# Tile shapes on TensorE in a two-block attention and convolution kernel: half-array score products, wide products as pairs of 64-column tiles

## The reference, cut to what matters

```python
# block 1, per image
xn  = layer_norm_over_channels(x_attn)            # first 48 of 192 channels
q, k, v = split(bn(w_qkv @ xn), (16, 16, 48))
attn = softmax(q.T @ k * 16**-0.5, axis=-1)       # 1024 x 1024
out  = v @ attn.T
y    = bn(w_proj @ relu(concat(out, x_skip)))
# block 2, per image
q, k, v = split(qkv_w @ x)                        # 8 heads of 24 channels
at   = softmax(l2norm(q) @ l2norm(k).T) @ v       # channel attention, 24 x 24 per head
conv = depthwise3x3(dw1 @ v)                      # conv1, conv2
t    = cp_in @ at                                 # 32 channels
cmap = cp_out @ (t * ci1(mean(t)) * ci2(t))       # 3x3, dilated 7x7, 1x1
smap = sp_out @ gelu_gate(depthwise3x3(sp_in @ conv))
y    = proj @ ((at + cmap) * sigmoid(smap) + conv * sigmoid(mean(cmap)))
```

## Time and profile before

| | |
|---|---|
| three timed runs | 395.29, 395.75, 396.08 us, median 395.75 |
| span of the profiled execution, first to last instruction | 393.8 us |
| what lies around the span, by the median | 1.95 us |
| PE busy, instructions | 353.9 us (90%), 2098 |
| DVE busy, instructions | 269.3 us (68%), 490 |
| ACT busy, instructions | 168.3 us (43%), 283 |
| POOL busy | 24.1 us |
| DMA | 12.37 MB, mean 31 GB/s |

### The profile page before, as it was taken

The page is one execution under the profiler, slowest core; times in us unless marked ns, Lnnn a source line. Parts: engine busy times, 40 slices in busy tenths (PEclk is TensorE's granted clock), DMA queues, the critical chain, the costliest instruction groups (busy, mean ns, idle before and its releaser), DMA issues.

```text
span 393.8 us, 5228 instructions
## 1 busy us (share of the span) xinstructions
PE 353.9 (90%) x2098; PEld 180.1 (46%) x2098; DVE 269.3 (68%) x490; ACT 168.3 (43%) x283; POOL 24.1 (6%) x29
## 2 busy tenths in 40 slices
PE   2978989999987998899999989998999889797995
PEld 1736644433465454544445465443244365352431
DVE  5757667551597647796878577889357889748553
ACT  2233054656503248346520775235522574625410
POOL 2030100000003200000000020000100001000000
PEclk9977689999997599999899999997999899969999
DMA  8450000000000001200002102000002111013005
GB/s 254 140 147 2 0 0 2 0 1 2 0 1 2 0 2 28 62 2 2 0 2 75 28 9 52 12 2 0 0 2 80 29 33 33 0 29 64 2 0 160
DMA packets 6069, 12.37 MB, mean 31 GB/s; under 512 B 2078, under 2 KB 2718, under 8 KB 5918
## 3 DMA queue, kind: packets, MB, share of 16 engines
q1 hardware_dynamic: 5532, 11.97, 11.2%
q10 hardware_dynamic: 514, 0.08, 0.1%
HBM read 5.32 MB, written 3.15 MB: 22 GB/s over the span
## 4 chain that ended last, share of the span: by engine, by line
PE 75%; ACT 7%; DVE 6%; SPq 4%; DMA 4%; POOL 2%; issue 1%; ACTq 0%
PE psO L616 5%; PE psR L791 5%; PE psA L606 4%; PE psA L587 3%; DVE nm L1374 2%; ACT pT L1980 2%; PE psB L659 2%; DMA x<-x_dram 2%; PE psB L680 2%; PE psS L616 2%; SPq L391 2%; DMA up<-up 2%; PE psA L564 2%; PE psA L791 2%; PE psO L544 2%
## 5 line engine op out<-in xcount | busy, mean ns | idle before, releaser
L1510 DVE SCALAR_TENSOR_TENSOR cx<-cpA,dw2w,cx 128x1024 f32<-128x1024 f32 x32 | 40.9, 1278 | 2.4 <-ACT cx L2012 2.4
L1521 DVE SCALAR_TENSOR_TENSOR dd<-spp,wt,dd 112x1024 f32<-112x1024 f32 x32 | 41.0, 1282 | 1.0 <-ACT dd L2093 0.3
L1980 ACT ACTIVATE pT<-psA 128x1024 f32<-128x1024 f32 x24 | 24.6, 1023 | 26.2 <-PE psA L606 26.0
L1374 DVE TENSOR_REDUCE nm<-psA 128x1 f32<-128x1024 f32 x20 | 24.5, 1223 | 12.2 <-PE psA L587 11.9
L616 PE MATMUL psO<-pT,vt 128*64 128x512 f32 x96 | 28.7, 678 | 0.1
L1510 DVE SCALAR_TENSOR_TENSOR cx<-cpB,dw2w,cx 128x512 f32<-128x512 f32 x32 | 23.8, 743 | 0.5 <-ACT cx L2012 0.5
L791 PE MATMUL psR<-up,wb 128*32 128x256 f32 (+1 forms) x336 | 20.9, 383 | 1.4 <-DMA up<-up 1.3
L606 PE MATMUL psA<-qs,ks 98*128 98x512 f32 x48 | 19.4, 488 | 2.1 <-ACT pT L1980 1.4
L587 PE MATMUL psA<-ks,qs 96*128 96x512 f32 x40 | 15.0, 456 | 3.2 <-DVE nm L1374 1.9
L606 PEld LDWEIGHTS psA<-qs,ks 98*128 98x128 f32 x48 | 8.1, 209 | 19.8 <-ACT pT L1980 16.2
L1310 DVE BATCH_NORM_STATS2 st<-x 128x6 f32<-128x512 f32 x24 | 15.7, 684 | 1.8 <-DMA x<-x_dram 1.6
(11 more groups left out here) (423 smaller groups left out, 735.9 us busy)
## 6 DMA issues: line engine op xcount, KB each, us to landing
up<-up SPq DMA_DIRECT2D x12, 200.0 KB, 3.1
x<-x_dram SPq DMA_DIRECT2D x4, 512.0 KB, 6.5
out_dram<-x SPq DMA_DIRECT2D x8, 256.0 KB, 2.1
wt<-params_dram SPq DMA_DIRECT2D x1, 1151.5 KB, 8.5
tp<-tp SPq DMA_DIRECT2D x8, 136.0 KB, 2.4
x<-x_dram SPq DMA_DIRECT2D x8, 128.0 KB, 5.0
out_dram<-x SPq DMA_DIRECT2D x8, 128.0 KB, 2.4
wt<-params_dram SPq DMA_DIRECT2D x1, 213.5 KB, 2.6
```

The costliest lines, as they stand in the source:

```text
L1374: v.tensor_reduce(s.nm[:, t:t + 1], score_ps[b][t % 2][:], AX_X, ALU.max, negate=True).then_inc(nm_s.of(b), 1)
L1510: v.scalar_tensor_tensor(acc, img, dw2w[:, blk, tap:tap + 1], acc, ALU.mult, ALU.add).then_inc(cv_s.of(c), 1)
L1521: v.scalar_tensor_tensor(acc, t.spp[:, dy:dy + HH, dx:dx + WW], par("w_spdw")[:, tap:tap + 1], acc, ALU.mult, ALU.add).then_inc(dv_s.of(c), 1)
L1980: a(s.pT[t % 2][:], s.scoreT_ps[:], ACT.Exp).then_inc(ex_s.of(b), 1)
```

## The change

Three things are done.

SP's order changes in one place: the stores of images 0 and 1 go behind `shift_u(1)` and `shift_t(2)`.

First, q and k are laid on 50 rows of each half of the array (rows 0 to 49 and 64 to 113): 2 rows for the maximum and 3 x 16 for high, low and high parts. q's half g holds the queries of pixels g x 512 and up, 512 columns; k stands in full in both halves. The two products of a `scores_t` step then lie in different array halves and write different banks. `score_rows` of images 2 and 3 does the same; of images 0 and 1 both products of a step use one half, and the next step the other. High and low parts are made on all rows at once by marks (`marks`, `mkb`) instead of on row slices. `row_max` of images 2 and 3 takes two partial maxima, and `split_max` joins them.

Second, `columns` issues each product with 128 (or 112) stationary columns as two products with 64.

Third, the 64-row parts of the projections become steps of their own (`_b`), as do the folded channels (`_last`), and all orders are listed anew.

```diff
+            def columns(o, w, x, start=True, stop=True):
+
+                half = o.shape[0] // 2
+                for j in range(2):
+                    p = slice(j * half, (j + 1) * half) if o.shape[0] == P else slice(j * SP2, min((j + 1) * SP2, o.shape[0]))
+                    last = mm(o[p], w[:, p], x, start=start, stop=stop, skip_group_check=True)
+                return last
...
+        def packed(g):
+            return slice(g * SP2, g * SP2 + 2 + 3 * QK)
...
-            t.qs = sb(f"qs_{i}", [P, N], F32R, on=on)
+            t.qs = sb(f"qs_{i}", [P, HB], F32R, on=on)
...
+            def q_product(b):
...
                 for n in range(2):
                     p = slice(n * SP2, n * SP2 + PD)
-                    last = mm(ps[0:CH, n * HB:(n + 1) * HB], w[p, :], s.xn[p, :], start=True, stop=True)
+                    last = mm(q_ps[b][rows(n), :], qw[p, rows(n)], s.xn[p, :], start=True, stop=True)
...
-            def score_rows(b, t):
...
-                for n in range(2):
-                    last = mm(ps[:, n * HB:(n + 1) * HB], s.qs[0:CH, t * P:(t + 1) * P],
-                              s.ks[0:CH, n * HB:(n + 1) * HB], start=True, stop=True)
+            def score_rows(b, j):
...
+                o = slice((j // 2) * P, (j // 2 + 1) * P)
+                if b < 2:
+                    p = packed(j % 2)
+                    for n in range(2):
+                        last = mm(score_ps[b][j % 2][:, n * HB:(n + 1) * HB], s.qs[p, o], s.ks[p, n * HB:(n + 1) * HB],
+                                  start=True, stop=True)
+                else:
+                    for g in range(2):
+                        p = packed(g)
+                        last = mm(psA[:, g * HB:(g + 1) * HB], s.qs[p, o], s.ks[p, (j % 2) * HB:(j % 2 + 1) * HB],
+                                  start=True, stop=True)
...
             def scores_t(b, t):
...
-                for n in range(2):
-                    last = mm(ps[:, n * HB:(n + 1) * HB], s.ks[0:CH + 2, t * P:(t + 1) * P],
-                              s.qs[0:CH + 2, n * HB:(n + 1) * HB], start=True, stop=True)
+                for g in range(2):
+                    p = packed(g)
+                    last = mm(ps[:, g * HB:(g + 1) * HB], s.ks[p, t * P:(t + 1) * P], s.qs[p, :], start=True, stop=True)
...
                 for v in range(2):
-                    mm(o[:, v, :, 0:4], gav[:, 0, v, :], s.mv[:, :, 0:4], start=True, stop=True)
-                    last = mm(o[:, v, :, 4:6], gav[:, 1, v, :], s.mv[:, :, 4:6], start=True, stop=True)
+                    columns(o[:, v, :, 0:4], gav[:, 0, v, :], s.mv[:, :, 0:4])
+                    last = columns(o[:, v, :, 4:6], gav[:, 1, v, :], s.mv[:, :, 4:6])
...
             def k_low(b):
...
-                v.scalar_tensor_tensor(s.ks[64:96, :], k_ps[64:96, :], bqk[64:96, 1:2], s.ks[64:96, :].bitcast(F32),
+                v.scalar_tensor_tensor(s.ks[:], k_ps[:], bkq[:, 0:1], s.ks[:].bitcast(F32),
...
             def max_copy(b):
...
-                a(s.qs[CH:CH + 2, :], s.max_ps[0:2, :], ACT.Copy).then_inc(qm_s.of(b), 1)
+                for g in range(2):
+                    a(s.qs[g * SP2:g * SP2 + 2, :], s.max_ps[0:2, g * HB:(g + 1) * HB], ACT.Copy).then_inc(qm_s.of(b), 1)
```

The orders, the few places that the prediction speaks of:

```diff
 # ACT
+            setup_ln()
             load_small()
-            setup_ln()
-            zero_front(0)
-            zero_back(0, 0)
...
 # DVE
+            setup_slot1()
             setup_zeros()
...
+            setup2_a()
+            group_stats(0, 0)
...
-            channel_stats(0, 2, 0)
             layer_norm(0)
...
             row_max(0, 4)
+            channel_stats(0, 2, 0)
+            row_max(0, 5)
```

More of the change, by code:

```diff
@@ L481, in setup_bias @@
                 pe.wait_ge(*gmm[0](0, 1))
[L482 to L483 removed]
+                for k, w in enumerate((kw, qw)):
+                    last = mm(psS[:, 500 + k:501 + k], w[:], par("pick_one"), start=True, stop=True)
                 last.then_inc(s_pe, 1)
@@ L535, in pixel_var @@
                 for t in range(4):
-                    last = mm(s.row_ps[:, 2 * t:2 * t + 2], s.sq[:, t * P:(t + 1) * P], par("mean_rows"),
-                              start=True, stop=True)
+                    last = columns(s.row_ps[:, 2 * t:2 * t + 2], s.sq[:, t * P:(t + 1) * P], par("mean_rows"))
                 last.then_inc(var_s.of(b), 1)
@@ L658, in conv1_a, with conv1_b, conv1_last @@
                 for n in range(2):
-                    mm(front.F[n], wc1[:, 0:P], pair[c % 2].X[:, n, :], start=True, stop=False)
+                    columns(front.F[n], wc1[:, 0:P], pair[c % 2].X[:, n, :], stop=False)
+            def conv1_b(c):
                 for n in range(2):
-                    last = mm(front.F[n], wc1B[rows(n), 0:P], pair[c % 2].X[rows(n), 2, :], start=False, stop=True)
+                    last = mm(front.F[n], wc1B[rows(n), 0:P], pair[c % 2].X[rows(n), 2, :], start=False, stop=True,
+                              skip_group_check=True)
                 last.then_inc(c1_s.of(c), 1)
-            def conv1_b(c):
+            def conv1_last(c):
                 pe.wait_ge(*ce_s(c, 1))
@@ L679, in gram_x @@
                 for k in range(NKT):
-                    last = mm(front.F[0][:, 0:C], front.xT[:, k, 0:P], front.xT[:, k, :], start=(k == 0), stop=(k == NKT - 1))
+                    last = columns(front.F[0][:, 0:C], front.xT[:, k, 0:P], front.xT[:, k, :], k == 0, k == NKT - 1)
                 last.then_inc(gp_s.of(c), 1)
@@ L689, in gram_w @@
                 for k in range(2):
-                    last = mm(front.F[0][:, 0:2 * C], front.gram[:, k, 0:P], wq[:, k, :], start=(k == 0), stop=(k == 1))
+                    last = columns(front.F[0][:, 0:2 * C], front.gram[:, k, 0:P], wq[:, k, :], k == 0, k == 1)
                 last.then_inc(tup_s.of(c), 1)
@@ L714, in k_norm_rows @@
                 for h in range(2):
-                    last = mm(front.F[1][0:CH, h * CH:(h + 1) * CH], ones[0:CH, :], front.dk[:, h, :], start=True, stop=True)
+                    for j in range(2):
+                        last = mm(front.F[1][rows(j), h * CH:(h + 1) * CH], ones[0:CH, 0:SP2], front.dk[:, h, :],
+                                  start=True, stop=True)
                 last.then_inc(kr_s.of(c), 1)
@@ L837, in attended_a, with attended_b @@
                 for n in range(2):
-                    mm(t.R[TAIL[n]], pair[c % 2].wmt[:, 0:P], pair[c % 2].X[:, n, :], start=True, stop=False, skip_group_check=True)
+                    columns(t.R[TAIL[n]], pair[c % 2].wmt[:, 0:P], pair[c % 2].X[:, n, :], stop=False)
+            def attended_b(c):
+                t = back[SLOT2[c]]
+                pe.wait_ge(*pr_s(c, 1))
                 for odd in range(2):
@@ L865, in proj2_a, with proj2_last @@
                 for n in range(2):
-                    mm(t.R[TAIL[n]], wph[:, 0:P], t.uu[:, n, :], start=True, stop=False)
-                for n in range(2):
-                    last = mm(t.R[TAIL[n]], wphB[rows(n), 0:P], t.uu[rows(n), 2, :], start=False, stop=True)
-                last.then_inc(op_s.of(c), 1)
+                    columns(t.R[TAIL[n]], wph[:, 0:P], t.uu[:, n, :], stop=False)
             def proj2_b(c):
                 t = back[SLOT2[c]]
+                for n in range(2):
+                    last = mm(t.R[TAIL[n]], wphB[rows(n), 0:P], t.uu[rows(n), 2, :], start=False, stop=True, skip_group_check=True)
+                last.then_inc(op_s.of(c), 1)
+            def proj2_last(c):
+                t = back[SLOT2[c]]
+                pe.wait_ge(*zz_s(c, 3))
+                pe.wait_ge(*ae_s(c, 3))
                 ps = t.R[TAIL[2]]
```

714 lines of the change are left out of this document (395 added, 319 removed).

## The result

The changed kernel takes 360.4 us (median of 4 runs, 359.1 to 363.8) where the kernel before took 395.5 beside it: ratio 0.913, 95% interval 0.907 to 0.919. It is 34.5 us faster. The forecast was 377 us and its range began at 366, so the direction was right and the size was not. The profiled execution has a span of 358.4 us.

What follows compares the result with a forecast made beforehand. PE's summed work in listed order was taken to bound the kernel. 393.8 - 19 (0.7 of PE's 27) + 0.8 - 0.4 = 375.2 us of span, plus 1.95: 377 us, range 366 to 391.

Steps and rivals of the forecast that it cites:

- What bounds the kernel: Whole kernel: bound by the sum of PE's work in its listed order, ACT and DVE entering where loops close.
- Part 1, half arrays: Score products on PE: pairs in different array halves overlap, 0.23 us less a scores_t step, together -11.1 us.
- Part 2, pairs with few columns: Wide products on PE with few moving columns, issued as pairs of 64-column tiles: together -10 us (bounds -5 and -12).
- the prediction's part 3: PE's listed orders: changes of tile shape fall from 232 to 197, at 0.175 us each, -6 us.
- Wide pairs at nothing: Wide products on PE with 512 moving columns: nothing is won by issuing them as pairs.
- Part 4: Other engines: q's parts cheaper but hidden; max_copy as two instructions +0.2 us an image, +0.8 on the path.
- Part 5, the start: Start on DVE and ACT: image 2's statistics later -1.8, loads later +2.2; sum -0.4 us (bounds -1.8 and +0.9).
- no DMA wait ahead of xn: Changed kernel's timeline at the start: a sign that would show the forecast of the start, with gav's copy at 7.2 to 9.7.
- How much reaches the end: Whole span: 0.7 of PE's 27 us saved arrives, -19 us (0.5: -13.5; all: -27).
- all of it arrives: Rival, whole kernel: new orders fill PE's waits and half-clock savings count double, 367 us or less; chance 0.13.
- The clock: Rival, slower: PE has more holes and the half level is granted longer, 403 us; sign 24 or fewer nines; chance 0.09.
- Reading PSUM sets the pace: Rival, softmax stages: row maxima and exponentials set the pace, so half-array scores save nothing, 387 us; chance 0.10.

Runs made afterwards that it cites:

- the run in the same half: The changed kernel with both products of every scores_t step taking their rows from half 0 of the array: 374.0 us, ratio 0.947.
- the scores alone: Orders of the kernel before, columns() issuing whole products, only the half-array scores left of the change: 392.5 us, ratio 0.985.
- the old orders: Changed kernel's products in the kernel before's orders on PE, DVE, ACT, SP: 374.1 us, ratio 0.944; with spare products in PE's gaps 372.4 us, 0.945.

## Why the prediction was wrong, point by point

**What bounds the kernel**: right. PE's sum set the time, and with the new orders what was taken from it arrived.

**Part 1, half arrays**: right in mechanism and size. 0.23 us a step is shown by the run in the same half. With the changes of shape that it brings (26 at 0.175, 4.6 us) -11.1 becomes -6.5; the scores alone brought 6.1. That the two agree so closely is luck, since the 6.1 can be 3 to 9.

**Part 2, pairs with few columns**: right that they win, size too small. Pairs are worth 16 to 17 us, 10 of it forecast; group means take 0.07 us a pass (16 instructions in 32.34 - 31.77 us) where 0.06 were forecast. Most of the rest stands in the prediction's part 3, which gave the net count (232 to 197; the trace before has 233) to the change as a whole. By the traces it is three terms: +26 from the half arrays, -45 from the pairs, -17 from the orders. The net of the first two is 3 us, and the pairs' own 8 were hidden behind the half arrays' cost. The price of a change itself, 0.175 us, fits both and is shown by neither alone. One reading is loose: 1.86 us for four passes of L616 are 0.465 each, and the 0.43 set beside them is the figure without the changes of shape.

**Wide pairs at nothing**: right within the noise. **Part 4**: the trace bears out what it priced on ACT: the two instructions of `max_copy` take 1.20 us where one took 1.01, +0.2 as forecast, and q's high part 0.78 for 1.11. No run singled it out.

**Part 5, the start**: wrong in one term. `gav` landed within the bounds (its copy at 8.12, forecast 7.2 to 9.7). "Which puts the start's other wait there" priced `setup2_a`'s wait at nothing. It was 3.91 us with `group_stats(0, 0)` queued behind it, and the start was 5.7 us later, where -0.4 was forecast; "no DMA wait ahead of xn" was wrong. The question to ask of a moved step was: who is queued behind a wait that moves ahead.

**How much reaches the end**: the step that failed. The prediction took 0.7 of all of PE's saved work, because "shortening uncovers the neighbours", and carried that share over to the new orders. With the old orders it held: from the xn of image 0 on, PE's busy time fell by 29.6 us and the time by 21.8, a share of 0.74, with PE's idle time up from 25.8 us to 33.7. With the new orders the busy time fell by 40.0 and the time by 41.2, with the idle time at 24.6: nothing was lost on the way.

**The orders**: the term that was missing, and the reason for the step above. The prediction priced the new lists by changes of shape alone, 3 us, and said nothing of the waits they close, which it named only in the rival "all of it arrives". They brought 12.5 us net of the start and some 18 without it. In the two traces from image 0's xn on they take 19.4 us: 9.1 of PE's idle time, and 10.4 of its busy time, of which most goes with 21.4 us less at half level (8 us at the ratio of rows 7). 12.5 less the 2 us (0.7 of 3) that they were given, and 5 that the products brought above 0.7 of the 24 us forecast for them (22 for 17, since they took 29.6 us off PE's busy time): that is nearly the whole gap of 16.6 us.

**The clock**: the rival had the wrong sign. The changed kernel had fewer, not more, stretches at half level: 36 slices with 9, not under 25. The fear that less work means more holes came true with the old orders (33.7 us of idle time for 25.8), where the half-level time still fell a little, from 54.9 us to 46.8. The new orders filled the holes, and it fell to 25.4. The forecast held the clock as it was but for 2 us in one rival; some 12 us of PE's busy time went with it.

**Reading PSUM sets the pace**: the loop of image 3 went from 1.85 to 1.62 us, of which ACT has 1.02, so part 1 counted in it. The Trainium skill (page "TensorEngine Tiling (Array Packing)", section "PSUM Bottleneck") says that the copies out of PSUM may become the bottleneck when the products get faster; they were not what decided here, though PE waits for ACT in it for 1.12 us at one step.

## What to carry to other kernels

Price a rewritten order by the waits it closes, not by its instructions alone, and give a share of what reaches the end for the new order, not for the old: list each engine's longest waits before, and ask of each whether the new list puts work there. Count changes of tile shape for each part of a change by itself, since a net count hides that one part pays for what another wins. And of any step that moves ahead in an engine's list, look up when the last thing that it waits for lands, and what is queued behind it.

## What was not expected of the hardware

- An fp32 product of one to eight moving columns is cheaper as two: for the norms (one column) a pair of 64-column tiles took 4.3/64 = 0.067 us, the whole product 7.6/64 = 0.119; for group means (four or eight) it was 0.57/8 = 0.07 for 0.88/8 = 0.11. One weight load takes 0.138 us with 64 columns and 0.192 with 128. Doubling the number of instructions made the kernel faster. That the two loads of a pair overlap would explain it and wasn't tested.
- Time at half level is not worth the same everywhere: 17 us of it cost 2 where DVE set the pace, and the loop of the run in the same half, which closes over PE's pair and ACT, went from 1.85 us a step to 3.05.
- Clearing one half-level stretch can bring another later in the same execution: in the old orders 15 us less in all gave no time back by the ratio (0.945 for 0.944). That the later stretches lie where PE is waited for would explain it and wasn't tested.
